# Attention stage of a one-core kernel: scores issued one head at a time, softmax maxima moved from Pool's queue straight into q's rows, q, k and v stored and loaded by fewer, longer DMAs

## The reference, cut to what matters

```python
q, k, v = heads(Wq, bq), heads(Wk, bk), heads(Wv, bv)      # B=8, H=16, T=1024, D=16
q, k = rope(q), rope(k)                                    # pairs of neighbouring dimensions
att = einsum('bhqd,bhkd->bhqk', q, k) / sqrt(D)
att = softmax(where(causal, att, -1e10), axis=-1)
y = einsum('bhqk,bhkd->bhqd', att, v)
out = x + y.reshape(B, T, C) @ Wp.T + bp
```

## Time and profile before

| | us |
|---|---|
| median of three runs (2920.36 to 3401.18) | 2934.43 |
| profiled execution, its own time | 2920.05 |
| its span, first to last instruction | 2918.3 |
| PE busy | 2265.9 (78%) |
| DVE busy | 1714.3 (59%) |
| ACT busy | 1193.3 (41%) |
| POOL busy | 946.5 (32%) |
| mean granted TensorE clock | 0.898 |

### The profile page before, as it was taken

One profiled execution on the slowest core, in us unless ns is written; L12 is line 12 of the kernel. 1 busy time (PEld: TensorE's weight loads), 2 busy tenths in 40 slices (PEclk: granted clock), 3 DMA queues, 4 the chain that ended last, 5 costly groups with the idle time before them and its releaser, 6 DMA issues. The chain is left out here.

```text
span 2918.3 us, 43437 instructions
## 1 busy us (share of the span) xinstructions
PE 2265.9 (78%) x14474; PEld 1446.1 (50%) x14475; DVE 1714.3 (59%) x5108; ACT 1193.3 (41%) x2467; POOL 946.5 (32%) x1248
## 2 busy tenths in 40 slices
PE   6579999644888888888888888889926540699997
PEld 6468888633333333333333333333315440588887
DVE  7345555332777677766776777767646650455553
ACT  1134444211355555555555555556611110344443
POOL 3624444155132223222222222210023427233342
PEclk9999999856799999999999999989966665799999
DMA  9452231126344535545445445443132102631320
GB/s 337 159 195 95 67 106 65 46 64 126 66 91 95 105 87 97 106 87 93 99 89 103 93 78 106 88 82 75 49 116 80 57 17 101 209 109 62 108 67 20
DMA packets 227559, 284.40 MB, mean 97 GB/s; under 512 B 21416, under 2 KB 171828, under 8 KB 225296
## 3 DMA queue, kind: packets, MB, share of 16 engines
q1 hardware_dynamic: 215056, 248.68, 34.6%
q0 software_dynamic: 12288, 33.05, 3.2%
HBM read 154.78 MB, written 127.66 MB: 97 GB/s over the span
## 5 line engine op out<-in xcount | busy, mean ns | idle before, releaser
L1619 ACT ACTIVATE at_probs<-at_score_ps 128x512 f32<-128x512 f32 (+3 forms) x1536 | 649.0, 494 | 521.7 <-PE at_score_ps L1735 380.2
L1498 DVE CUSTOM_DVE_ANT_0 at_junk<-at_max_ps,at_causal 128x128 f32<-128x128 f32 (+3 forms) x1024 | 491.1, 486 | 230.3 <-PE at_max_ps L1720 224.2
L1732 PE MATMUL at_score_ps<-at_q,at_k 99*128 99x512 bf16 (+3 forms) x1536 | 449.1, 337 | 86.8 <-ACT at_probs L1619 48.7
L1720 PE MATMUL at_max_ps<-at_k,at_q 96*128 96x512 bf16 (+3 forms) x1536 | 456.6, 342 | 9.7 <-DVE at_peak L1501 5.9
L1501 DVE TENSOR_REDUCE at_peak<-at_max_ps 128x1 f32<-128x512 f32 x512 | 352.2, 688 | 153.8 <-PE at_max_ps L1720 151.5
L1021 DVE TENSOR_TENSOR f_hid_lo<-f_hid,f_hid_hi 128x512 fp32r<-128x512 f32 x256 | 177.3, 693 | 323.4 <-ACT f_hid_hi L1047 322.9
L1745 PE MATMUL at_o_ps<-at_probs,at_v 128*32 128x512 f32 (+3 forms) x3072 | 340.6, 516 | 0.1
L1085 PE MATMUL f_y_ps<-f_w_hi,f_hid_hi 128*128 128x256 f32 x1024 | 292.8, 286 | 43.7 <-DVE f_xe L997 28.9
L1044 ACT ACTIVATE f_hid<-f_hid_ps 128x512 f32<-128x512 f32 x256 | 153.3, 599 | 412.9 <-PE f_hid_ps L1070 412.9
L1720 PEld LDWEIGHTS at_max_ps<-at_k,at_q 96*128 96x128 bf16 x1536 | 129.7, 99 | 349.4 <-DVE at_peak L1498 146.3
L1085 PE MATMUL f_y_ps<-f_w_hi,f_hid_lo 128*128 128x256 f32 x1024 | 291.3, 285 | 0.0
(11 more groups left out here) (179 smaller groups left out, 3700.9 us busy)
## 6 DMA issues: line engine op xcount, KB each, us to landing
f_w_raw<-in_w SPq DMA_DIRECT2D x32, 1024.0 KB, 7.7
qk<-at_part SPq DMA_DIRECT2D x96, 256.0 KB, 2.9
at_q<-qk SPq DMA_DIRECT2D x192, 128.0 KB, 4.9
at_k<-qk SPq DMA_DIRECT2D x192, 128.0 KB, 7.7
expert_in<-r_zeros SPq DMA_DIRECT2D x16, 1040.0 KB, 15.9
f_xe<-expert_in SPq DMA_DIRECT2D x32, 520.0 KB, 8.3
v_rows<-at_v_out SPq DMA_DIRECT2D x64, 256.0 KB, 3.6
at_v<-v_rows SPq DMA_DIRECT2D x32, 512.0 KB, 9.9
```

Of the source, the lines that this page charges most:

```text
L1498: v.tensor_tensor_reduce(junk[bank(k, r)][:, 0:w], src, causal[:, HALF - w:HALF], 1.0, LEAST, ALU.add, ALU.max, out).then_inc(max_used, 1)
L1619: a.activation(probs[t % 2][:, h, c0:c0 + w], score_ps[(GH * t + h) % BANKS][:, 0:w], ACT.Exp, scale=float(SCALE)).then_inc(exp_done, 1)
L1720: te.matmul(max_ps[bank(u, r)][:, 0:w], q[u][0:ROWS, h, i * P:(i + 1) * P], kk[u][0:ROWS, h, k0:k0 + w], start=True, stop=True).then_inc(m ...
L1732: last = te.matmul(out[:, 0:w], kk[u][:, h, j * P:(j + 1) * P], q[u][:, h, hf * HALF + c0:hf * HALF + c0 + w], start=True, stop=not diagonal)
```

## The change

- `scores` handles one head. In each share c of a step PE issues head c's scores of step t+1 first, then the pieces of preparation, `times_v` at c=2, then the maxima's products.
- The channels of q and k are reordered (dimension outside, head inside, within a group of four heads), in the weights, the biases and Pool's views in `rope`, whose cosine and sine are now read with a stride of 0 innermost. A DRAM row block of one part and one group is then 16 dimensions of four heads, 8 KB for each dimension.
- `qk` is one DRAM tensor [batch, part, 512, 1024]; one DMA stores all three parts of a pair (768 KB), one stores v of both tiles (512 KB, runs of 1 KB in place of 512 bytes).
- q is loaded by three DMAs and k by three: copies of parts (0,1,2), (0,1), (0) and (0,1), (0,1), (0,2). The same six products are summed. The source view of a DMA is [parts, 16, 4096], the destination 16 partitions for each part.
- The maxima's tiles are laid out so that three parts times four heads are 12 rows. PE transposes four times, 128x12 to 12x128, in place of once; DVE copies 12x512 in place of 48x128; DVE's copy waits for the landing of the other half's move in place of the store. Pool issues one DMA from `peak_t` (12 rows of 512) to q's rows 96 to 98. Pool does the move of the first half at step 6, that of the second half at the end of the body, ahead of the sine stage of `rope` at step 0 of the next.

```diff
-K_PARTS = (0, 1, 0, 2, 0, 1)
-Q_PARTS = (0, 0, 1, 0, 2, 1)
+Q_RUNS = ((0, 1, 2), (0, 1), (0,))
+K_RUNS = ((0, 1), (0, 1), (0, 2))
@@ store_pair
-                for a in range(PARTS):
-                    sp.dma_start(dr["qk"][a][bass.ds(b * 2 * C, 2 * C), bass.ds(i * 2 * P, 2 * P)]
-                                 .rearrange("(c p) t -> p c t", p=P), part[a][:]).then_inc(stored, 16)
-                for s in range(2):
-                    sp.dma_start(dr["v"][bass.ds(b * NG, NG), :, bass.ds(2 * i + s, 1), :]
-                                 .rearrange("g p a c -> p (g a) c"),
-                                 v_out[s][:].rearrange("p (g h) c -> p g (h c)", g=NG)).then_inc(stored, 16)
+                sp.dma_start(dr["qk"][b, :, :, i * 2 * P:(i + 1) * 2 * P]
+                             .rearrange("a (c p) t -> p (a c) t", p=P),
+                             parts[:].rearrange("p a c t -> p (a c) t")).then_inc(stored, 16)
+                sp.dma_start(dr["v"][b * NG:(b + 1) * NG, :, 2 * i:2 * i + 2, :].rearrange("g p s c -> p g (s c)"),
+                             v_outs[:].rearrange("p g s h c -> p g (s h c)")).then_inc(stored, 16)
@@ load_group
-                for dst, parts, r0 in ((q, Q_PARTS, 0), (kk, K_PARTS, C)):
-                    for c, a in enumerate(parts):
-                        sp.dma_start(dst[u][c * D:(c + 1) * D, :, :],
-                                     dr["qk"][a][bass.ds(b * 2 * C + i * GH * D + r0, GH * D), :]
-                                     .rearrange("(h d) t -> d h t", d=D)).then_inc(qkv_loaded[u], 16)
+                for dst, runs, r0 in ((q, Q_RUNS, 0), (kk, K_RUNS, C)):
+                    at, row = 0, i * GH * D + r0
+                    for run in runs:
+                        stride = run[1] - run[0] if len(run) > 1 else 1
+                        sp.dma_start(dst[u][at:at + len(run) * D, :, :],
+                                     dr["qk"][b, run[0]:run[-1] + 1:stride, row:row + GH * D, :]
+                                     .rearrange("a (d h) t -> a d (h t)", d=D)).then_inc(qkv_loaded[u], 16)
+                        at += len(run) * D
@@ move_peaks, now in Pool's block
-                wait_apart(sp, max_used, at + BANKS + 1, sh.passed)
-                sp.dma_start(dr["peaks"][half].rearrange("a (r c) -> (a r) c", c=P), peak_t[:]
-                             ).then_inc(peak_stored, 16)
-                wait_apart(sp, peak_stored, 16 * (2 * g + half + 1), sh.passed)
-                sp.dma_start(q[u][ROWS:ROWS_M, :, half * HALF:(half + 1) * HALF],
-                             dr["peaks"][half].rearrange("a (h t) -> a h t", t=HALF)).then_inc(peak_loaded[half], 16)
+                wait_apart(pool, max_used, at + BANKS + 1, sh.passed)
+                p.dma_start(q[u][ROWS:ROWS_M, :, half * HALF:(half + 1) * HALF], peak_t[:]
+                            ).then_inc(peak_loaded[half], 16)
@@ rope
-                    return a[:, table, :].rearrange("p a d -> p (a d)").unsqueeze(1).to_broadcast([P, 2 * H, D])
+                    return (a[:, table, :].rearrange("p a d -> p (a d)").unsqueeze(1).unsqueeze(3)
+                            .to_broadcast([P, 2 * NG, D, GH]))
@@ Pool's loop body
+                    if t == 6 and more:
+                        move_peaks(g + 1, slot_round(g, k, 1)[0], 0)
...
+                if more:
+                    move_peaks(g + 1, slot_round(g, k, 1)[0], 1)
@@ DVE, ring
-                    dve.wait_ge(peak_stored, 16 * (2 * whose + half))
+                    dve.wait_ge(peak_loaded[1 - half], 16 * (whose + half))
@@ PE, ring
-                    te.transpose(peaks_in_ps(u, r), peak_part[:].rearrange("p a h i -> p (a h i)"), sh.ident_bf[:]
-                                 ).then_inc(max_ready, 1)
+                    for i in range(TPB // 2):
+                        last = te.transpose(peaks_in_ps(u, r)[:, i * P:(i + 1) * P],
+                                            peak_part[:, i].rearrange("p a h -> p (a h)"), sh.ident_bf[:])
+                    last.then_inc(max_ready, 1)
@@ PE's loop body
                     for c in range(SHARES):
+                        if t + 1 < NS:
+                            scores(g, k, t + 1, c)
+                        elif more:
+                            scores(g + 1, slot_round(g, k, 1)[0], 0, c)
                         piece(c)
-                        if c < 2:
-                            if t + 1 < NS:
-                                scores(g, k, t + 1, c)
-                            elif more:
-                                scores(g + 1, slot_round(g, k, 1)[0], 0, c)
                         if c == 2:
                             times_v(g, k, t)
                         places(c)
@@ scratch and inputs
-        "qk": [dram(f"qk{a}", [B * 2 * C, S], BF16) for a in range(PARTS)],
+        "qk": dram("qk", [B, PARTS, 2 * C, S], BF16),
+    def dims_first(a):
+        return np.ascontiguousarray(a.reshape(a.shape[:-1] + (NG, GH, D)).swapaxes(-1, -2).reshape(a.shape))
```

More of the change, by code:

```diff
@@ L1153, in attention_block @@
         rot = [sb(f"rot{k}", [P, 2 * C], F32) for k in range(2)]
-        part = [sb(f"part{k}", [P, 2 * CC, 2 * P], BF16) for k in range(PARTS)]
+        parts = sb("parts", [P, PARTS, 2 * CC, 2 * P], BF16)
+        part = [parts[:, a] for a in range(PARTS)]
         rest = [sb(f"rest{k}", [P, 2 * CC, P], F32) for k in range(2)]
[L1156 to L1161, removed]
+        v_outs = sb("v_outs", [P, NG, 2, GH, VW], F32)
+        v_out = [v_outs[:, :, k] for k in range(2)]
+        peak = [sb(f"peak{k}", [P, TPB // 2, GH], F32) for k in range(2)]
+        peak2 = sb("peak2", [P, TPB // 2, GH], F32)
+        peak_rest = sb("peak_rest", [P, TPB // 2, GH], F32)
+        peak_part = sb("peak_part", [P, TPB // 2, PARTS, GH], BF16)
+        peak_t = sb("peak_t", [PARTS * GH, HALF], BF16)
         o_out = [sb(f"o_out{k}", [P, HALF], F32) for k in range(2)]
@@ L1327, in body @@
                     load_group(g + 2, slot_round(g, k, 2)[0])
-                if more:
-                    move_peaks(g + 1, slot_round(g, k, 1)[0], 0)
-                    move_peaks(g + 1, slot_round(g, k, 1)[0], 1)
                 store_o(g, 1)
@@ L1376, in third_parts, with move_peaks @@
                                 ALU.subtract).then_inc(part2_ready, 1)
+            def move_peaks(g, u, half):
+                at = place(g, RING.index(FIRST)) if half == 0 else place(g + 1, RING.index(SECOND))
+                wait_apart(pool, max_used, at + BANKS + 1, sh.passed)
+                p.dma_start(q[u][ROWS:ROWS_M, :, half * HALF:(half + 1) * HALF], peak_t[:]
+                            ).then_inc(peak_loaded[half], 16)
             invert_std(0)
@@ L1390, in _ @@
             rope(LEAD - 1, 1, 0)
+            move_peaks(0, 0, 0)
+            move_peaks(0, 0, 1)
             def body(g, k, more, prepare, finish):
@@ L1462, in add_bias_v @@
                 for s in range(2):
-                    last = v.tensor_tensor(v_out[s][:, :, 0:D],
-                                           prep_ps[:, s * C:(s + 1) * C].rearrange("p (h d) -> p h d", d=D),
-                                           bias[:, 2 * C:3 * C].rearrange("p (h d) -> p h d", d=D), ALU.add)
+                    last = v.tensor_tensor(v_out[s][:, :, :, 0:D],
+                                           prep_ps[:, s * C:(s + 1) * C].rearrange("p (g h d) -> p g h d", d=D, h=GH),
+                                           bias[:, 2 * C:3 * C].rearrange("p (g h d) -> p g h d", d=D, h=GH), ALU.add)
                 last.then_inc(v_ready, 1)
@@ L1494, in ring @@
                 wait_apart(dve, max_ready, place(g, r) + 1, sh.passed)
-                out = (peak2 if k0 else peak[half])[:, h, i:i + 1]
+                out = (peak2 if k0 else peak[half])[:, i, h:h + 1]
                 src = max_ps[bank(k, r)][:, 0:w]
@@ L1721, in ring, with scores @@
                           start=True, stop=True).then_inc(max_ready, 1)
-            def scores(g, u, t, pr):
+            def scores(g, u, t, h):
                 c0, w, diagonal = columns(STEPS[t])
                 hf, j = STEPS[t]
-                if t in FIRST_STEP.values() and pr == 0:
+                if t in FIRST_STEP.values() and h == 0:
                     pe.wait_ge(peak_loaded[hf], 16 * (g + 1))
-                for h in range(2 * pr, 2 * pr + 2):
-                    pe.wait_ge(exp_done, GH * (NS * g + t) + h + 1)
-                    out = score_ps[(GH * t + h) % BANKS]
-                    last = te.matmul(out[:, 0:w], kk[u][:, h, j * P:(j + 1) * P],
-                                     q[u][:, h, hf * HALF + c0:hf * HALF + c0 + w], start=True, stop=not diagonal)
-                    if diagonal:
-                        last = te.matmul(out[:, 0:P], sh.ident_bf[:], hide_bf[:], start=False, stop=True)
-                    last.then_inc(score_ready, 1)
+                pe.wait_ge(exp_done, GH * (NS * g + t) + h + 1)
+                out = score_ps[(GH * t + h) % BANKS]
```

(15 more changed lines are left out.)

40 lines of the change are left out of this document (16 added, 24 removed).

## The result

The changed kernel takes 3339.07 us (median of four runs, 3335.13 to 3341.81) where the kernel before took 2928.39 beside it: ratio 1.141 [1.137, 1.145], slower by 14%. One of the four runs of the kernel before took 3401.18 us, far off the other three (2920.36 to 2934.43); the ratio leaves it out. The profiled execution's span is 3336.8 us for 2918.3. Forecast: 3411, range 3250 to 3600.

What follows compares the result with a forecast made beforehand. Bound by a circle through its own loads, which the change puts on two or three DMA engines: 2920.05 + 416.1 (groups 0 to 26) + 43.6 (last four) + 31.2 (prologue) = 3411 us, range 3250 to 3600.

Steps and rivals of the forecast that it cites:

- What bounds the kernel before: Main loop: a circle of first score, store, load, maxima, first score, 44.6 us a group; PE stops 32.4 us in all.
- The mechanism: q and k loads: outermost count limits a transfer's DMA engines, 3 for the first q DMA, 2 for four others.
- o_in load's 8: Load with 8 outermost into 128 partitions: no landing, DMA share 0.52 at 161 GB/s, half of the engines.
- Rate and beginning of the load: Store to load's landing: 24.5 GB/s an engine, load 28.4 us, 1 to start, 1 to land; 35.1 with the store.
- rival 1: Group loads: few engines and slow ones, 20.1 GB/s, 34.6 us a load; 3609 us in all, chance 0.16.
- First score to store: Each group, first score to pair's first store: 24.9 us always instead of 20.7, the clock being low after PE's stop.
- rival 2: Group start: few engines, but the clock holds, 20.7 for 24.9 us; 3286 us in all, chance 0.14.
- Scores by head and the transposes: First score to store: transposes cost 0 to 1.2 us, scores gain 0 to 2.8; together 0, ends -50 and +35.
- Last four: Last four groups: three still load at 48.0 us each, the fourth loads nothing; 182.0 for 138.4, +43.6 us.
- Prologue: Before the first score: two loads of 28.4 us delay the store DVE waits for, 722.46 to 753.7, +31.2 us.
- Rivals 3 and 4, the wide case: Loads stay on 16 engines: 2880 us, chance 0.08; or also Pool's rotation late: 2934 us, chance 0.02.

Runs made afterwards that it cites:

- e6: The kernel before with scores issued one head at a time, nothing else changed: 2853.61 us, ratio 0.976.
- e7: The kernel before with only the change's maxima move (four transposes, 12 rows, Pool's queue straight to q): 2886.0 us, ratio 0.986.
- e11: The kernel before with scores by head and the maxima's move from Pool's queue, its transfers untouched: 2811.97 us, ratio 0.958.
- e1: The changed kernel with q and k loaded as twelve transfers of one part each, 16 dimensions outermost: 2782.36 us, ratio 0.951.
- e10: The kernel of e1 with the loads' DRAM view reordered to eight outermost, [8, 2, 4096], which can't be merged: 2811.95 us, ratio 0.957.
- e9: The kernel of e1 with the loads' DRAM view reordered to four outermost, [4, 4, 4096], which can't be merged: 2932.69 us, ratio 0.998.
- e2: The changed kernel with the same number of q and k transfers and bytes, but 16 dimensions outermost in the DRAM view: 2765.77 us, ratio 0.945.
- e4: The kernel of e2 with scores issued two heads at a time again: 2872.07 us, ratio 0.981.
- e12: The changed kernel with scores issued two heads at a time as before: 3421.39 us, ratio 1.166.
- e5: The kernel of e2 with the maxima's moves back on SP's queue behind the loads, still straight to q: 2760.64 us, ratio 0.944.
- e8: The kernel of e1 with the loads' DRAM side written as [4, 4, 4096], which was merged back to 16 outermost: 2781.25 us, ratio 0.951.
- e3: The changed kernel with q's three-part transfer split into one of two parts and one of one part: 3282.18 us, ratio 1.121.

## Why the prediction was right, and where its terms were off

**What bounds the kernel before: right.** The circle first score, store, load, maxima, first score was there. e6 shortened one link, first score to store, from 21.1 to 19.2 us; the way from store to first score stayed (23.4, then 23.3), and the stops grew from 32 to 80 us. e7 took the maxima's way through SP and DRAM out, and they fell to 9. What I missed is how near a second limit lay, the order of the scores: with both gone (e11) the loop gains 122.9. Waits for a score bank are 42 to 46 us of what the order is worth; what makes up the rest isn't shown.

**The mechanism: right, and it is shown.** By outermost count of the q and k loads, 16, 8, 4, then 3 and 2, the period is 39.9, 40.2, 44.4, 57.7 (e1, e10, e9, after). A stretch inside one load of q and k, of e1, e10, e9 and after in this order:

```profile
1297.00:1304.00 7.00, 6.98 (x49) 3.42 (x48) 5.38 (x15) 4.42 (x8) 3.29 (x4) 1.00 1.05 146
1320.00:1324.00 4.00, 3.98 (x30) 2.33 (x29) 3.56 (x11) 2.77 (x6) 1.77 (x3) 1.00 0.52 154
1387.00:1393.00 6.00, 5.72 (x33) 2.06 (x25) 4.48 (x11) 3.26 (x7) 0.00 (x0) 1.00 0.26 107
1517.00:1528.00 11.00, 0.00 (x0) 0.00 (x0) 0.25 (x2) 0.00 (x0) 0.00 (x0) 0.69 0.13 53
```

The DMA share is 16, 8, 4 and 2 sixteenths. Eight engines move as much into the 16 partitions of a transfer as sixteen do (with sixteen, e1, a packet of 8 KB took some 940 ns, with eight some 500), which is why e10 loses next to nothing; with four and two the rate falls to 107 and 53 GB/s. A whole load, first issue to last semaphore event, takes 17.4, 18.4, 22.1 and 35.3 us (medians from the records of the trace). e2 has the same few transfers as after with 16 outermost and loses nothing. For that step, from the o_in load's 8 down to 3 and 2, I had only an inference. The Trainium skill (DMA: Bandwidth & Descriptors, "Why a DMA increments its semaphore by 16 and not by 1") gives the rule, the largest divisor of the outermost counts up to 16. The shares above agree with it at 16, 8, 4 and 2, and the semaphore events of e9 and e10, 5 and 9 for each load, stand one above the 4 and 8.

**Rate and beginning of the load: two sizes off, cancelling in part.** I took 24.5 GB/s for one engine, 28.4 us. In the trace an 8 KB packet of an engine that is served alone takes 313 ns, 26.2 GB/s, so 26.6 us: the best end of my bounds, and far from rival 1's 20.1. The two microseconds for beginning and landing were too few: load issue to first score is 35.3 us, and after 3.3 for the rest of the store's 4.7 and 26.6 for bytes, 5.4 remain. Most of that is slow packets at the start: between 1501.1 and 1501.5 they took 0.9 to 1.1 us each, and over groups 3 to 26 the first 48 packets of 8 KB, those of the first transfer, have a mean of 525 ns, the next 32, of the second, 460, the rest 315. At 16 packets for an engine and transfer that is 3.4 and 2.3 us over the 313 ns, an estimate, since the means are over all engines. Pair store to first score came to 57.66 - 20.08 = 37.6, for 35.1: +2.5 a group. In e9 the same remainder is 22.2 - 3.3 - 16.3 = 2.6, and the first 32 packets have a mean of 333 ns: it isn't a constant.

**First score to store: the step that failed.** "So I take 24.9 always" stood on one group of before, whose low clock began when PE started again. After, the clock falls within the stop (1521 of 1516 to 1533) and is back at 1.00 at 1538, so most of the low stretch passes while PE stands. All 30 stops look alike: the granted clock is at 0.50 from 1.8 to 5.0 us behind the stop's beginning until 3.2 to 6.4 us behind its end, where in before, after the stop of 2.67 us, it stayed at 0.50 for 12.5 us of work. Measured is 20.1. Scores by head take 1.8 to 2.1 off before's 21.1 (e2 against e4, e6, e12), so the clock costs about 1.1 us, from 20.1 against e1's 19.0, and not 4.2. This is also why rival 2, in which the clock holds, was nearer than it deserved (3286): the clock fell in every group and cost little.

**Scores by head and the transposes, taken together as 0**, with -50 as the one end: -55.4 for the scores alone in the stopped loop (e12 against after).

**The sum: part of its closeness is luck.** Loop: 27 x (57.66 - 60.0) = -63 against the forecast; made up of 27 x (20.1 - 24.9) = -130 and 27 x (37.6 - 35.1) = +67. Last four: +36.9 for +43.6. Prologue: +30.0 for +31.2; its 2 x 28.4 of load were measured in DVE's wait of 48.4 us (I said near 45). Two terms of the loop, 130 and 67 us off, pulled against each other; with the stretch from first score to store alone put right the sum would have been some 3280.

**Rivals 3 and 4, the wide case.** Its condition, a load under some 18 us, held barely: first issue to last semaphore event is 17.4 us in e1 and 15.9 in e2 (16.4 before), and in e1 the first score follows that event by only 0.5 us. The circle through the loads is thus nearly tight still. e5 shows that SP's queue serves the maxima as well. Its price was wrong: 2880 is what e4 takes, 2872, but with scores by head, as in the change, it is 2766. Pool's slack was about enough: in the main loop of e2 no wait of PE is put down to Pool's `at_rot`; the weight loads of the product that reads it (L1707) stand 8.8 us in all, 21 times and at most 0.4 us, with no releaser named.

**Where the 5.5% of e2 come from**, in ratios: maxima's move and scores by head 4.2 (e11), new stores, layout and 8 KB rows together 0.7 (e1 against e11), six loads for twelve 0.6 (e2 against e1). The last two are 13.6 and 11.6 us of the loop, near the width of the intervals; the parts of the 0.7 were not run apart. Fewer and longer transfers are thus worth a little when they stay wide. As written in the change they gave all gains back and 411 us more.

## What to carry to other kernels

Read a DMA by the outermost dimension of both sides before its bytes and runs: folding several copies into one transfer must not put the small count outermost. On SP's queue a missing landing in the list of issues is the sign to look for; then read the DMA share of a stretch inside the load, for eight engines (no landing either, e10) cost next to nothing here, and two or three cost 18 us a group. A dimension that is contiguous with its neighbour was merged and did not count (e8). Where a kernel is a circle through a load, test a removed wait together with the next limit under it: e6 and e7 alone gave 93 us, together 123.

## What the runs showed that I had not expected

- The same transfer of three rows has 16 semaphore events from Pool's queue (landing 4.5 us) and 4 from SP's (none shown, e5). It isn't wider for that: in the packet records of e1 each of Pool's moves is three packets of 4 KB with the data and 13 of 16 bytes. On Pool's queue a landing doesn't tell how many engines carry data. Loads of q and k from Pool's queue were not tried.
- On SP's queue the semaphore events in the trace are the outermost count and one: 3, 4, 5 and 9 for 2, 3, 4 and 8 (the 3 from e3: 63 for a group's load, less 16 of v and 32 of two wide ones, over five transfers). In a move of e5 issued at 1343.31 the first of the four came 1.16 us after the issue, before the data's packets (1.4 to 1.6 us), the other three at 2.2. The first event is therefore no sign that any data has landed.
- Over the 27 groups a long stop, with the clock's low stretch mostly inside it, cost PE about 1.1 us of slow matmuls (20.1 us against e1's 19.0), where one of 2.67 us in before had cost 4.2.
